# The order of VectorE's work in a time-mix stage, and a rotary cross product as one GpSimd operation

## The chip, the core and the metric

The kernel runs on one core of one Trainium2 chip. Its engines run side by side, each in the order of its own program: PE (matmuls), DVE (VectorE), ACT (ScalarE), POOL (GpSimd) and SP, which here only issues DMAs. They wait for one another through semaphores. The metric is the device time of the launch in microseconds (us), the median of several runs. Times below that look like 1041.29 are us from the start of the profiled span.

## What is computed

One sequence x of 2048 tokens by 128 channels, float32, goes through two parts:

```python
x = layernorm(x + time_mix(x))        # RWKV-6: a recurrence with a decay per channel, 2 heads of 64
x = layernorm(x + layers(x))          # 6 layers of local attention and a gated MLP

# time_mix: y_t = r_t S + (r_t u k_t) v_t ;  S = exp(-exp(w_t)) S + k_t v_t ;  then a norm by head, a gate, @ Wo
# each of the 6 layers, 16 heads of 64, window 32:
q = l2norm(q) * q_scale ; k = l2norm(k) * k_scale
q = q * cos * scale + rotate_half(q) * sin * scale      # k with 1 / scale
x = softmax(8 q k', masked to the window) v @ Wo + x
x = a * gelu(gate) @ W2 + b2 + x
```

rotate_half swaps the two halves of each head's 64 channels and changes the sign of one. The sign lies in the kernel's table of sines, so what is left is a product of each half with a table, written to the other half's place.

## The kernel before

All data stay in SBUF. There are three blocks of code: time_mix (up to about 205 us), layers (up to about 2015 us) and last_norm.

**time_mix** works on 4 groups of 512 tokens (4 chunks of 128). Its loop has 6 steps, and one step treats up to three groups at once: m, whose inputs are mixed and projected; g = m - 1, whose coefficients within a chunk are made level by level; and e = m - 2, whose outputs are made, normed, gated and added. Each engine has this step written out by hand in one order, and that order is what the first part of the change touches on DVE (lines 515 to 624). The operations that matter, in DVE's order before:

- scale_level(g, 0) to (g, 6), L492 to L498: r, k and the decays are scaled for the next level. PE multiplies level by level (L650), so they alternate. Behind level 6 PE transposes k (L794), ACT copies it with the far coefficients (L455 to L457), and PE makes the products that are added to the states (L808).
- stream(0) to (4), L504; cut, L554: the levels' products by masks, 2 x 768 elements.
- y_sum, y_c, y_var, y_eps, y_n, y_w, y_g (L531 to L571): the norm and gate of group e. PE turns y_g (L774), ACT copies it, PE multiplies by Wo (L799).
- res, res_sum, res_c (L576 to L582): the output of e plus x, less its mean. It waits for PE's L799.
- coef (L590): two sums over the levels of cut. PE needs them in the next step (L718).
- gate (L595): from ACT's gate_t (L438). POOL makes gate_w and gate_b from it (L383), and PE may write the bank again.
- res_var, res_eps (L600, L603): from ACT's squares (L461). POOL takes them to the power -0.5 (L377).
- mixed_input(m + 1): xx and x_mixed (L509, L513), the input of the next group. The first matmuls of PE's next step (L687, L689) read it; the first also waits until ACT's rate (L442) has read the bank.
- state (L617), 8 operations: the 4 chunks' states one after the other. They wait for PE's L808. PE's levels 0 and 1 of the next step overwrite the banks that the states read, so they wait for all 8.
- x_tok (L622): the normed output of e. PE turns it (L680) in the next step, after levels 0 and 1.

**layers** works on 96 tiles (6 layers by 16 tiles of 128 tokens), software-pipelined: in step s the projections of tile p = s + 1, the scores of tile a = s and the outputs of tile b = s - 1. The MLP takes two tiles together, so odd and even steps differ, and the unrolled loop holds one of each. For a tile PE projects q and k (L1282, L1297); ACT squares them (L1056); DVE sums (L1153), makes the inverse roots in nine small operations (L88 to L104) and multiplies, unit[0] and unit[1] (L1178). PE's v projection (L1354) overwrites q's bank, so it waits for unit[0]. DVE's root operations come behind heads_out (L1159), which waits for PE's L1316 of tile b. Of the rotation, POOL makes for q: across in two halves (L1000), along (L1034), rotated (L1008); then for k: across, rotated; DVE makes k's along (L1236). POOL goes on with the next table, turns (L1019), and the shifted inputs (L988, L989, L1027, L1028). PE transposes rotated (L1249). One order of POOL for all of it; `cross` and `add_turned` are the two functions that the second part touches.

Of the kernel before, what the change touches and what calls it, by code (L numbers as in the profile page):

```python
# [26 lines left out]
ALU = mybir.AluOpType  # L27
ACT = mybir.ActivationFunctionType
AX = mybir.AxisListType
# [36 lines left out]
def after(engine, semaphore, count):  # L66

    if not isinstance(count, int) or count > 0:
        engine.wait_ge(semaphore, count)
# [124 lines left out]
def time_mix(nc, ctx, given):  # L194
# [20 lines left out]
    with ExitStack() as own:  # L215
# [105 lines left out]
        with nc.Block() as block:  # L321
# [147 lines left out]
            def _(dve):  # L469
# [30 lines left out]
                def step(m, g, e):  # L500
# [71 lines left out]
                    if g is not None:  # L572
                        scale_level(g, 6)
                    if e is not None:
# [10 lines left out]
                    if g is not None:  # L585
                        dve.wait_ge(s_cut, 2 * g + 2)
                        after(dve, s_y, g)
                        for pair in range(2):
                            part = slice(4 * pair, 4 * pair + 4)
                            dve.tensor_reduce(coef[:, part, :], cut[:, part, :, :].rearrange("p a l t -> p a t l"),  # L590
                                              AX.X, ALU.add).then_inc(s_coef, 1)
                    if m is not None:
                        dve.wait_ge(s_gt, m + 1)
                        after(dve, s_gb, m)
                        dve.scalar_tensor_tensor(gate[:, :, :], gate_t[:, :, :], 1.0,  # L595
                                                 slots[:, 1, :].rearrange("p (c d) -> p c d", c=CHUNKS_G),
                                                 ALU.add, ALU.mult).then_inc(s_gate, 1)
                    if e is not None:
                        dve.wait_ge(s_rsq, e + 1)
                        dve.tensor_reduce(res_var[:, :], res_sq[:, :, :], AX.X, ALU.add).then_inc(s_rvar, 1)  # L600
                        dve.wait_ge(s_rvar, e + 1)
                        after(dve, s_pow2, e)
                        dve.tensor_scalar(res_eps[:, :], res_var[:, :], LN_EPS, None, ALU.add).then_inc(s_reps, 1)  # L603
                    if m is not None and m + 1 < GROUPS:
                        mixed_input(m + 1)
                    if g is not None:
# [3 lines left out]
                        for c in range(CHUNKS_G):  # L610
# [3 lines left out]
                            for h in range(R_HEADS):  # L614
# [4 lines left out]
                                                         ALU.mult, ALU.add).then_inc(s_state, 1)  # L619
                    if e is not None:  # L620
# [933 lines left out]
```

## Time and profile before

| | |
|---|---|
| median of 3 runs | 2035.73 us (2034.1 to 2036.3) |
| the profiled execution | 2036.49 us, of it 2034.7 in the span |
| PE | 1804.0 us busy (89%) |
| DVE | 1578.9 us busy (78%) |
| POOL | 1480.6 us busy (73%) |
| ACT | 1163.4 us busy (57%) |
| POOL across (L1000) | 384 operations of 128x512, 524.6 us, mean 1386 ns |
| POOL rotated (L1008) | 192 operations of 128x1024, 495.8 us, mean 2582 ns |
| PE waits for POOL's rotated | 56.1 us, 51 times |
| PE's v projection waits for DVE's unit | 24.2 us, 47 times |

A line of a timeline gives the start, the time taken, the engine, the line of code, the operation and what it writes and reads; "x8" means that eight like it in a row are put together. In square brackets stands how long the engine had been idle before it and what ended that: "[6.08 <-DVE x_mixed L513]" is 6.08 us of idle time that ended when DVE's line 513 was done. "issue" means that the profile shows nothing that it waited for. A share of busy time doesn't say which engine sets the pace where all of them wait for each other in turn; for that one follows who released whom.

### The profile page before, as it was taken

To read this page: it belongs to the slowest core of one execution; us is meant where nothing else is said; L and a number is where in the kernel's file an instruction comes from. 1 tells how busy PE (TensorE), PEld (TensorE's weight loads), DVE (VectorE), ACT (ScalarE), POOL (GpSimd) and SP (SyncE) were. 2 spreads that over 40 slices of the span, in tenths; PEclk is the share of its full clock that TensorE was granted. 3 is DMA by queue.
4 is the path that set the end of the run, shared out by engine and by line. 5 is a ranking of instruction groups with operands and counts; after the bars stand their busy time and mean duration, and the time that the engine had idled before them with its cause. 6 is when DMAs were issued, how large, how long until landed. Compare 5 with 4: busy or idle time off the path is not lost. (4 is left out here: it accounts for less than half of the span.)

```text
span 2034.7 us, 85964 instructions
## 1 busy us (share of the span) xinstructions
PE 1804.0 (89%) x34280; PEld 1309.1 (64%) x34280; DVE 1578.9 (78%) x2776; ACT 1163.4 (57%) x1966; POOL 1480.6 (73%) x1159
## 2 busy tenths in 40 slices
PE   7774689999999999999999999999999999999985
PEld 3443367767666667666666666666766666666664
DVE  3665588888888888888888888888888888888874
ACT  2221356656666666666666666656656666666663
POOL 3221588788887887888877878788788877887871
PEclk8786799999999999999999999999999999999998
DMA  4000122223222223222223222223222232222220
GB/s 148 2 3 1 42 61 61 55 58 93 66 64 56 62 58 83 66 73 59 54 53 93 66 68 53 61 62 91 63 63 62 54 84 68 73 56 52 57 62 22
DMA packets 93581, 123.43 MB, mean 61 GB/s; under 512 B 27760, under 2 KB 41808, under 8 KB 93392
## 3 DMA queue, kind: packets, MB, share of 16 engines
q1 hardware_dynamic: 93232, 122.42, 23.9%
q8 instruction: 46, 0.75, 0.2%
q10 hardware_dynamic: 288, 0.13, 0.0%
q14 instruction: 15, 0.12, 0.0%
HBM read 20.74 MB, written 1.05 MB: 11 GB/s over the span
## 5 line engine op out<-in xcount | busy, mean ns | idle before, releaser
L1000 POOL TENSOR_TENSOR across<-unit,turns 128x512 f32<-128x512 f32 x384 | 524.6, 1386 | 266.1 <-issue 254.5
L1008 POOL TENSOR_TENSOR rotated<-along,across 128x1024 f32<-128x1024 f32 x192 | 495.8, 2582 | 20.4 <-POOL along L1034 9.6
L1153 DVE TENSOR_REDUCE sums<-squares 128x16 f32<-128x1024 f32 x192 | 234.1, 1219 | 157.3 <-ACT squares L1056 151.2
L1249 PE MATMUL turn<-identity,rotated 128*128 128x128 f32 x1536 | 205.0, 277 | 56.1 <-POOL rotated L1008 56.1
L1249 PEld LDWEIGHTS turn<-identity,rotated 128*128 128x128 f32 x1536 | 172.5, 141 | 118.7 <-issue 101.5
L1034 POOL TENSOR_TENSOR along<-unit,turns 128x1024 f32<-128x1024 f32 x96 | 227.3, 2368 | 0.0
L1354 PE MATMUL proj_a<-w_qkv,shift_a 128*128 128x512 f32 x384 | 190.1, 618 | 34.3 <-DVE unit L1178 24.2
L1115 ACT COPY val<-proj_a 128x1024 f32<-128x1024 f32 x96 | 97.2, 1012 | 179.2 <-PE proj_a L1354 179.2
L1091 ACT COPY k_t<-turn 128x512 f32<-128x512 f32 x192 | 103.2, 589 | 155.0 <-PE turn L1249 155.0
L1379 PEld LDWEIGHTS att<-o_t,w_o 128*128 128x128 f32 x1536 | 186.4, 192 | 6.0 <-issue 1.0
L1282 PE MATMUL proj_a<-w_qkv,shift_a 128*128 128x512 f32 x384 | 183.5, 601 | 4.3 <-POOL shift_a L988 3.0
L1379 PE MATMUL att<-o_t,w_o 128*128 128x128 f32 x1536 | 186.9, 275 | 0.0
L1236 DVE TENSOR_TENSOR along<-unit,turns 128x1024 f32<-128x1024 f32 x96 | 182.8, 1904 | 0.0
L1297 PE MATMUL proj_b<-w_qkv,shift_a 128*128 128x512 f32 x384 | 181.1, 594 | 0.0
L1056 ACT ACTIVATE squares<-proj_a 128x1024 f32<-128x1024 f32 x96 | 98.3, 1024 | 114.2 <-PE proj_a L1282 114.2
L1342 PEld LDWEIGHTS turn<-k_t,q_t 64*32 64x32 f32 x12288 | 129.0, 105 | 42.1 <-issue 41.8
L1316 PE MATMUL att<-v_win,p_t 64*32 64x64 f32 x12288 | 154.1, 225 | 0.8 <-ACT p_t L1076 0.8
L1076 ACT COPY p_t<-att 128x512 f32<-128x512 f32 x192 | 103.2, 589 | 89.8 <-PE att L1249 89.8
L1316 PEld LDWEIGHTS att<-v_win,p_t 64*32 64x32 f32 x12288 | 135.9, 105 | 19.6 <-issue 17.1
L1159 DVE TENSOR_TENSOR heads_out<-att,inv_mass 128x512 f32<-128x512 f32 x192 | 123.6, 686 | 29.7 <-PE att L1316 29.7
L1342 PE MATMUL turn<-k_t,q_t 64*32 64x64 f32 x12288 | 145.1, 227 | 0.1
L1170 DVE TENSOR_TENSOR logits<-turn,row_max 128x512 f32<-128x512 f32 x192 | 132.7, 691 | 6.6
(203 smaller groups left out, 3448.9 us busy)
## 6 DMA issues: line engine op xcount, KB each, us to landing
v_win<-val SPq DMA_DIRECT2D x1536, 64.0 KB, 2.0
w_qkv<-wqkv_dram SPq DMA_DIRECT2D x18, 512.0 KB, 4.0
w_o<-wo_dram SPq DMA_DIRECT2D x6, 512.0 KB, 5.2
where<-positions_dram SPq DMA_DIRECT2D x1, 2048.0 KB, 10.2
w_ffn<-ffn_dram SPq DMA_DIRECT2D x12, 170.5 KB, 2.3
w_ffn<-ffn_dram SPq DMA_DIRECT2D x6, 192.0 KB, 2.3
x_tok<-x_dram SPq DMA_DIRECT2D x4, 256.0 KB, 4.2
out_dram<-final SPq DMA_DIRECT2D x4, 256.0 KB, 2.4
```

Of the source, the lines that this page charges most:

```text
L1000: pool.tensor_tensor(a[:, :, 1 - half, :], u[:, :, half, :], table, ALU.mult)\
L1008: pool.tensor_tensor(rotated[j][:, :, :], along[j][:, :, :], across[j][:, :, :], ALU.add).then_inc(rotated_in[j], 1)
L1034: pool.tensor_tensor(along[0][:, :, :], unit[0][:, :, :], turns[mine][:, 0, :].unsqueeze(1).broadcast_to([128, HEADS, HEAD]), ALU.mult).th ...
L1153: dve.tensor_reduce(sums[:, j, :], squares[j][:, :, :], AX.X, ALU.add).then_inc(summed[j], 1)
L1236: dve.tensor_tensor(along[1][:, :, :], unit[1][:, :, :], turns[mine][:, 2, :].unsqueeze(1).broadcast_to([128, HEADS, HEAD]), ALU.mult).the ...
L1249: mm = pe.transpose(bank[:, TILE * (i % 4):TILE * (i % 4) + TILE], buffer[:, TILE * i:TILE * i + TILE], identity[:, :])
L1282: mm = pe.matmul(bank_a[:, half, :], shift_a[mine][:, :], w_qkv[:, 512 * half:512 * half + 512], start=True, stop=True)
L1297: mm = pe.matmul(bank_b[:, half, :], shift_a[mine][:, :], w_qkv[:, base:base + 512], start=True, stop=True)
L1316: mm = pe.matmul(bank_s[WINDOW * w:WINDOW * w + WINDOW, par, HEAD * a_:HEAD * a_ + HEAD], p_t[rows, a_, WINDOW * w:WINDOW * w + WINDOW], v ...
L1342: mm = pe.matmul(bank_t[WINDOW * w:WINDOW * w + WINDOW, par, HEAD * a_:HEAD * a_ + HEAD], q_t[rows, a_, WINDOW * w:WINDOW * w + WINDOW], k ...
L1354: pe.matmul(bank_a[:, par, :].rearrange("p (a e) -> p a e", a=PAIRS), shift_a[mine][:, :], values[:, par, :, :], start=True, stop=True).th ...
L1379: mm = pe.matmul(bank_s[:, 0, 0:TILE], w_o[:, a_, :], o_t[:, a_, :], start=(a_ == 0), stop=(a_ == PAIRS - 1))
```

## The change

Two parts. In time_mix's step DVE makes coef ahead of scale_level(g, 6) and, behind that level, mixed_input(m + 1) and gate; then res, res_sum and res_c; then the states; and res_var and res_eps come behind the states, directly ahead of x_tok. In layers' rotation the two halves of across become one operation on 1024 elements, whose output is written with the two halves in reverse order; its semaphore rises by 1 for a tile instead of 2, and the waits on it are changed to match.

```diff
--- before.py
+++ after.py
@@ -570,7 +570,22 @@
                         after(dve, s_yturn, e)
                         dve.tensor_tensor(y_g[:, :, :], y_w[:, :, :], gate_b[e % 2][:, :, :], ALU.add).then_inc(s_yg, 1)
                     if g is not None:
+                        dve.wait_ge(s_cut, 2 * g + 2)
+                        after(dve, s_y, g)
+                        for pair in range(2):
+                            part = slice(4 * pair, 4 * pair + 4)
+                            dve.tensor_reduce(coef[:, part, :], cut[:, part, :, :].rearrange("p a l t -> p a t l"),
+                                              AX.X, ALU.add).then_inc(s_coef, 1)
+                    if g is not None:
                         scale_level(g, 6)
+                    if m is not None and m + 1 < GROUPS:
+                        mixed_input(m + 1)
+                    if m is not None:
+                        dve.wait_ge(s_gt, m + 1)
+                        after(dve, s_gb, m)
+                        dve.scalar_tensor_tensor(gate[:, :, :], gate_t[:, :, :], 1.0,
+                                                 slots[:, 1, :].rearrange("p (c d) -> p c d", c=CHUNKS_G),
+                                                 ALU.add, ALU.mult).then_inc(s_gate, 1)
                     if e is not None:
                         dve.wait_ge(s_out, e + 1)
                         dve.tensor_tensor(res[:, :, :], turn[:, 1, :].rearrange("p (c d) -> p c d", c=CHUNKS_G),
@@ -582,27 +597,6 @@
                         dve.scalar_tensor_tensor(res_c[:, :, :],
                                                  res_sum[:, :].unsqueeze(2).broadcast_to([128, CHUNKS_G, DIM]),
                                                  -1.0 / DIM, res[:, :, :], ALU.mult, ALU.add).then_inc(s_rc, 1)
-                    if g is not None:
-                        dve.wait_ge(s_cut, 2 * g + 2)
-                        after(dve, s_y, g)
-                        for pair in range(2):
-                            part = slice(4 * pair, 4 * pair + 4)
-                            dve.tensor_reduce(coef[:, part, :], cut[:, part, :, :].rearrange("p a l t -> p a t l"),
-                                              AX.X, ALU.add).then_inc(s_coef, 1)
-                    if m is not None:
-                        dve.wait_ge(s_gt, m + 1)
-                        after(dve, s_gb, m)
-                        dve.scalar_tensor_tensor(gate[:, :, :], gate_t[:, :, :], 1.0,
-                                                 slots[:, 1, :].rearrange("p (c d) -> p c d", c=CHUNKS_G),
-                                                 ALU.add, ALU.mult).then_inc(s_gate, 1)
-                    if e is not None:
-                        dve.wait_ge(s_rsq, e + 1)
-                        dve.tensor_reduce(res_var[:, :], res_sq[:, :, :], AX.X, ALU.add).then_inc(s_rvar, 1)
-                        dve.wait_ge(s_rvar, e + 1)
-                        after(dve, s_pow2, e)
-                        dve.tensor_scalar(res_eps[:, :], res_var[:, :], LN_EPS, None, ALU.add).then_inc(s_reps, 1)
-                    if m is not None and m + 1 < GROUPS:
-                        mixed_input(m + 1)
                     if g is not None:
                         dve.wait_ge(s_add, g + 1)
                         dve.wait_ge(s_scaled, 3 * LEVELS * (g + 1))
@@ -617,6 +611,12 @@
                                 dve.scalar_tensor_tensor(new[part, part], old[part, part], decay[LEVELS - 1][part, c:c + 1],
                                                          chunk_bank(c)[part, at:at + R_HEAD],
                                                          ALU.mult, ALU.add).then_inc(s_state, 1)
+                    if e is not None:
+                        dve.wait_ge(s_rsq, e + 1)
+                        dve.tensor_reduce(res_var[:, :], res_sq[:, :, :], AX.X, ALU.add).then_inc(s_rvar, 1)
+                        dve.wait_ge(s_rvar, e + 1)
+                        after(dve, s_pow2, e)
+                        dve.tensor_scalar(res_eps[:, :], res_var[:, :], LN_EPS, None, ALU.add).then_inc(s_reps, 1)
                     if e is not None:
                         dve.wait_ge(s_pow2, e + 1)
                         dve.tensor_tensor(x_tok[:, CHUNKS_G * e:CHUNKS_G * e + CHUNKS_G, :], res_c[:, :, :],
@@ -994,16 +994,14 @@
                     pool.wait_ge(united[j], p + 1)
                     after(pool, rotated_in[j], p)
                     u, a = halves(unit[j]), halves(across[j])
-                    for half in range(2):
-                        table = turns[odd][:, 2 * j + 1, 32 * half:32 * half + 32].unsqueeze(1).broadcast_to(
-                            [128, HEADS, 32])
-                        pool.tensor_tensor(a[:, :, 1 - half, :], u[:, :, half, :], table, ALU.mult)\
-                            .then_inc(acrossed[j], 1)
+                    table = turns[odd][:, 2 * j + 1, :].rearrange("p (two e) -> p two e", two=2).unsqueeze(1)\
+                        .broadcast_to([128, HEADS, 2, HEAD // 2])
+                    pool.tensor_tensor(a[:, :, ::-1, :], u, table, ALU.mult).then_inc(acrossed[j], 1)
 
                 def add_turned(j, p):
 
                     pool.wait_ge(alonged[j], p + 1)
-                    pool.wait_ge(acrossed[j], 2 * p + 2)
+                    pool.wait_ge(acrossed[j], p + 1)
                     after(pool, (q_turned, k_turned)[j], 2 * p)
                     pool.tensor_tensor(rotated[j][:, :, :], along[j][:, :, :], across[j][:, :, :],
                                        ALU.add).then_inc(rotated_in[j], 1)
@@ -1014,7 +1012,7 @@
                     p, mine = s + 1, 1 - odd
                     if live["p"]:
                         after(pool, alonged[1], p - 1)
-                        after(pool, acrossed[1], 2 * (p - 1))
+                        after(pool, acrossed[1], p - 1)
                         after(pool, alonged[0], p - 1)
                         pool.tensor_tensor(turns[mine][:, :, :], where[:, tile_of(p), :, :], scales[:, layer_of(p), :, :],
                                            ALU.mult).then_inc(table_made, 1)
@@ -1174,7 +1172,7 @@
                     def unite(j):
                         dve.wait_ge(rooted, ROOT_OPS * p + ROOT_OPS)
                         after(dve, alonged[j], p)
-                        after(dve, acrossed[j], 2 * p)
+                        after(dve, acrossed[j], p)
                         dve.tensor_tensor(unit[j][:, :, :], by_head((bank_a, bank_b)[j]),
                                           inv_norm[:, j, :].unsqueeze(2).broadcast_to([128, HEADS, HEAD]),
                                           ALU.mult).then_inc(united[j], 1)
```

## Rows read from the trace of the kernel before

**Rows 1.** Windows view, layers: stretch, length, busy us of each engine (instructions).

```profile
300.00:1980.00 1680.00, 1567.22 (x30254) 1155.06 (x30252) 1378.26 (x2372) 1060.06 (x1778) 1360.26 (x1049) 1.00 0.26 65
```

**Rows 2.** Timeline, PE, layers: start us, us, engine, line, operation, out<-in, count [idle before].

```profile
1027.30 1.96 PE L1354 MATMUL proj_a<-w_qkv,shift_a 128*128 128x512 f32 x4 [0.61 <-DVE unit L1178]
1041.29 1.09 PE L1249 MATMUL turn<-identity,rotated 128*128 128x128 f32 x8 [0.99 <-POOL rotated L1008]
1043.83 1.49 PE L1342 MATMUL turn<-k_t,q_t 64*32 64x64 f32 x128
1045.40 1.53 PE L1354 MATMUL proj_a<-w_qkv,shift_a 128*128 128x512 f32 x3
```

**Rows 3.** Timeline, DVE, layers: the first tiles and two steady tiles.

```profile
231.11 2.29 DVE L88 SCALAR_TENSOR_TENSOR sums_min<-sums 128x32 f32<-128x32 f32 x1
...
1007.22 1.22 DVE L1178 TENSOR_TENSOR unit<-proj_a,inv_norm 128x1024 f32<-128x1024 f32 x1
...
1040.51 1.29 DVE L1159 TENSOR_TENSOR heads_out<-att,inv_mass 128x512 f32<-128x512 f32 x2 [0.30 <-PE att L1316]
1042.16 0.32 DVE L92 TENSOR_TENSOR root_work<-inv_norm 128x32 f32<-128x32 f32 x1
1043.08 0.19 DVE L98 SCALAR_TENSOR_TENSOR inv_norm<-root_work,inv_norm 128x32 f32<-128x32 f32 x1
1044.08 1.23 DVE L1178 TENSOR_TENSOR unit<-proj_a,inv_norm 128x1024 f32<-128x1024 f32 x1
```

**Rows 4.** Timeline, POOL, layers, the same steady tiles.

```profile
1042.15 0.28 POOL L988 COPY shift_a<-xa 64x128 f32 x1 [0.30 <-POOL turns L1019]
1045.44 2.49 POOL L1000 TENSOR_TENSOR across<-unit,turns 128x512 f32<-128x512 f32 x2 [2.66 <-issue]
1047.89 2.37 POOL L1034 TENSOR_TENSOR along<-unit,turns 128x1024 f32<-128x1024 f32 x1
```

**Rows 5.** View of one line (L383): line, engine, operation, count: ns min/median/max, starts; form.

```profile
L383 POOL TENSOR_TENSOR gate_w<-gate,half_rows x4: 1261/1453/1657, 26.9 to 144.7; 128x512 f32<-128x512 f32 x4
```

**Rows 6.** Timeline, PE, first stage: operations behind the long idle stretches.

```profile
29.11 1.22 PE L687 MATMUL att<-x_mixed,w 128*128 128x512 f32 x1 [2.63 <-DVE x_mixed L513]
...
103.83 1.22 PE L687 MATMUL att<-x_mixed,w 128*128 128x512 f32 x1 [6.08 <-DVE x_mixed L513]
...
146.29 0.34 PE L650 MATMUL proj_a<-rf_bonus,kf 64*32 64x32 f32 x14 [6.04 <-DVE state L617]
...
147.81 0.48 PE L680 MATMUL turn<-identity,x_tok 128*128 128x128 f32 x1
...
169.04 0.48 PE L794 MATMUL proj_a<-identity,kf 128*128 128x128 f32 x1 [0.99 <-DVE decay L498]
...
180.84 0.48 PE L680 MATMUL turn<-identity,x_tok 128*128 128x128 f32 x1 [7.48 <-DVE x_tok L622]
```

**Rows 7.** Timeline, DVE, first stage, the step m=2, g=1, e=0 and the next step's start.

```profile
86.42 0.69 DVE L571 TENSOR_TENSOR y_g<-y_w,gate_b 128x512 f32<-128x512 f32 x1
89.44 0.42 DVE L492 TENSOR_TENSOR rf<-rf,decay 128x256 f32<-128x256 f32 x1 [2.32 <-PE proj_b L781]
...
98.18 2.81 DVE L590 TENSOR_REDUCE coef<-cut 128x128 f32<-128x768 f32 x2
104.94 1.22 DVE L617 SCALAR_TENSOR_TENSOR state<-state,decay,proj_b 64x64 f32<-64x64 f32 x4
106.19 0.69 DVE L622 TENSOR_TENSOR x_tok<-res_c,rstd 128x512 f32<-128x512 f32 x1
108.90 0.43 DVE L492 TENSOR_TENSOR rf<-rf,decay_one 128x256 f32<-128x256 f32 x1 [2.02 <-PE proj_b L650]
```

**Rows 8.** Timeline, ACT, first stage: rate in step m=0, the copies of far in step m=1.

```profile
26.52 0.69 ACT L442 ACTIVATE rate<-att,vec 128x512 f32<-128x512 f32 x1 [0.46 <-PE att L790]
...
55.28 0.52 ACT L455 COPY far<-proj_a 32x128 f32<-32x128 f32 x2
```

**Rows 9.** Timeline, POOL, first stage: the power behind the variance of res, step m=3.

```profile
143.73 1.02 POOL L377 TENSOR_TENSOR rstd<-res_eps,minus_half 128x4 f32<-128x4 f32 x1 [17.26 <-DVE res_eps L603]
```

## The prediction

> **What bounds the kernel now.** I read three views. First the busy times by stretch: in the layers PE is busy 93% of the time, at a granted clock of 1.00 [rows 1]. Its gaps are small, so the question is which of them set the pace. That is read from the engines' timelines over two tiles, one after the other; the pattern repeats every 36.86 us, which is two tiles: DVE's first unit operation starts at 1007.22 and again at 1044.08, with the one of the other tile between them [rows 3].
>
> Follow the loop that closes. PE projects v at 1045.40, 0.09 after DVE's first unit operation ends (1044.08 + 1.23 = 1045.31) [rows 2, 3]. From there PE runs almost without a gap to the products of probabilities and values. In the tile before, their end is what releases DVE's division (heads_out) at 1040.51, after 0.30 of idle; then come nine small root operations and unit at 1044.08 [rows 3], and PE's next v projection waits for that. In the other tile the same wait is seen as 0.61 of idle PE behind unit [rows 2]. So the pace is PE -> heads_out -> root -> unit -> PE, and **POOL is not in this loop**.
>
> POOL seems to be in it: PE waits 0.99 for the rotated keys at 1041.29 [rows 2]. But what follows that wait, the score products, ends at 1043.83 + 1.49 = 1045.32, and the v projection behind it waits for unit until 1045.31 anyway. The two chains meet within 0.1 us. If POOL is earlier, PE idles the same time a little further on; if POOL is later by more than 0.1, it sets the pace.
>
> The first stage, which lasts to about 205 us, is another matter: each engine waits for the others in turn. PE stands idle for 2.63, 6.08, 6.04 and 7.48 us in front of operations that wait for x_mixed, x_mixed, the states and x_tok [rows 6]. All four are DVE's, and DVE makes all four behind work that nobody waits for yet. That is what the first part of the change moves.
>
> **Part 1, DVE's order in the first stage.** A step treats three groups of 512 tokens at once: m (inputs), g (levels), e (outputs). The same instructions are issued as before; only their order changes, with the waits that they have. No DMA, PE, ACT or POOL instruction moves. Step by step (m = 0, 1, 2, 3, none, none):
>
> Step m=0. x_mixed of group 1 was made behind gate and released PE at 29.11 [rows 6]. It now comes ahead of gate, in an idle stretch of DVE, and is ready before gate was. PE's first product must still wait until rate has left its bank: ACT's rate runs from 26.52 to 27.21 [rows 8]. So PE starts at about 27.3 instead of 29.1: **-1.8**. The bounds are 1.5 and the whole idle, 2.6.
>
> Step m=1. Here the coefficient sums (2.81 for the two [rows 7]) come ahead of level 6, whose keys PE transposes for ACT to copy. But ACT starts these copies at 55.28 with no idle before them, right behind its other work [rows 8], so most of the delay is covered. I take **+0.2** for what sticks out; if no cover held it would be up to 2. x_mixed of group 2 is early here too, but PE had no gap at that place.
>
> Step m=2. DVE ends y_g at 86.42 + 0.69 = 87.11 and level 6 started at 89.44, after PE had released it [rows 7]. The sums fill this hole: 87.1 + 2.8 = 89.95, level 6 is 0.5 late, and its transposes come later than that anyway, since two PE products lie ahead of them. Then x_mixed of group 3 is ready at about 92.2, gate at 92.9, and res to res_c stay where they are, since they wait for PE; they end where the sums began, at 98.2 [rows 7]. Now the states follow at once: PE had their products done at 103.83 - 6.08 = 97.75 [rows 6]. They take 2 x 1.25 [rows 7]: 98.25 to 100.75. Then the variance of res (0.7 + 0.2), POOL's power (1.0 [rows 9]) and x_tok (0.69 [rows 7]): 103.45. DVE's level 0 of the next step started at 108.90 [rows 7] and now starts at 103.45. PE, which no longer waits at 97.75, has its two input products and levels 0 and 1 done at 102 to 103, and then waits for x_tok to turn it. That turn stood at about 108.8 and is at 103.5: **-5.3**. Thus the 6.08 of idle is not all won: what is late next is x_tok, whose power on POOL used to hide beside the states and now is bare. Bounds 4.3 and 6.1.
>
> Step m=3. There is no further input. PE had the states' products done at 146.29 - 6.04 = 140.25 [rows 6]. States 140.3 to 142.8, variance to 143.7, power to 144.7, x_tok to 145.45. PE turned x_tok at 147.81 [rows 6], now at 145.5: **-2.3**. The levels alone could start 3.5 earlier; again x_tok is last. Bounds 1.5 and 3.5.
>
> Step g=3. PE waits here for level 6 already (0.99 of idle at 169.04 [rows 6]), so the sums ahead of it cost their 0.5 in full, in the output products and in res. What DVE then leaves out between res_c and x_tok is the 2.8 of sums; but the power, 1.0, comes bare: 2.8 - 1.1 - 0.5 = 1.2, and rounding the semaphores down, **-1.1** on the turn that stood at 180.84 [rows 6]. Bounds 0.5 and 1.7. The last step has nothing that moved.
>
> Sum of part 1: -1.8 + 0.2 - 5.3 - 2.3 - 1.1 = **-10.3**. PE's clock goes up and down in this stage; I count nothing for that, and 2 either way in the range.
>
> **Part 2, the cross product as one operation.** It takes out one of two POOL operations, twice in each of 96 tiles, and one semaphore increment. A pair spans 2.49, and the along operation next to it, with as many elements as both halves (1024) and a broadcast table too, takes 2.37 [rows 4]. So a merged operation should save 0.12. No row shows its exact form, with three free dimensions and one of them backwards. The nearest: a half (16 runs of 32) takes half of 2.49 plus the overlap, some 1.26, and gate_w, of as many elements in 4 runs of 128, takes 1.261 at its quickest [rows 5]. So the number of runs costs nothing, and I take 2.37. The bounds are 2.3 and, if something in the form costs, 2.37 x 1.5 = 3.5.
>
> Twice 0.12 puts POOL's second rotated 0.25 earlier, and by the loop above that is worth nothing: PE waits 0.74 instead of 0.99 for the keys, and longer for unit. Two small things are left. POOL's copy of shift_a (0.28) lies over the root operations, and DVE's root operation at 1042.16 takes 0.32 beside it, where one behind it takes 0.19 [rows 3, 4]; two root operations a tile are hit so, 0.13 each, and these are on the loop. Moved up by 0.25, the copies still lie over root operations. What each hit costs depends on which starts first, so a part of the 0.26 may go in one of the two tiles: 0 to 0.2 for each pair of tiles, times 44 pairs (48 less the filling): 0 to -9, and I take **-2**. And while the layers fill, in the first tiles, DVE's root operation waits out POOL's rotated operation (2.29 instead of 0.19 at 231.11 [rows 3]), so POOL is on the path there: two times 0.12 in a tile or two, **-0.5**.
>
> A longer operation also holds DVE off for longer. The Trainium skill (SBUF — State Buffer, section "Who interferes with whom") says that POOL and a DVE operation with two SBUF inputs exclude each other for a whole instruction. By that rule a DVE operation issued under the merged product can wait 2.37 where it waited 1.26. The wait at 231.11 agrees with it. In the steady tiles no such DVE operation is issued while a cross product runs, so by the rule nothing would be added there.
>
> **Sum.** The profiled execution took 2036.49 (span 2034.7), the median is 2035.73. 2036.49 - 10.3 - 2 - 0.5 = 2023.7; from the median the same 12.8 gives **2022.9**.
>
> **The rivals.**
> *The stage gives back.* Group 0 to 3 are chained by many waits, and I followed only those that I saw end last. If in two of the steps another wait ends next, 4 or so is left of 10.3: 2035.7 - 5 = 2031. For it: x_tok turns up as next in three steps already. Against: the idle stretches are long and the moved operations have their inputs.
> *POOL's wait is the pace.* If PE's 0.99 at 1041.29 was the true limit, each pair of tiles gains 0.25: 44 x 0.25 = 11, and the time is 2012. Against it stands the meeting of the two chains at 1045.3.
> *The copies leave the root operations.* 0.2 for each pair: 9 instead of 2, the time is 2016.
> *The merged product is slower than the pair* (the other side). For y more than 2.49 each, two lie in a row in POOL's chain, which has 0.1 of slack in every second tile. The cost is 44 x (2y - 0.1); it eats the 10.8 of the rest from y = 0.17 on, a merged operation of 2.66. At 3.5, y = 1.0, it is +84: 2109; at y = 0.3 it is +22: 2047. For it: the form is unseen. Against: runs cost nothing in the rows. The Trainium skill (GPSIMD Engine Reference, section 7) has a rule of +50% for reads whose step is over 8 bytes; by its words it doesn't bite, since the innermost step stays 4 bytes and the backward step is in the output, and no run so far shows more.
> *The merge saves nothing* (2.49 as before): the fill and the copies stay, and the time is 2025, inside my forecast.
>
> **How the numbers follow.** Forecast, with the last of these: 0.60. Gain in the steady tiles by POOL's pace or by the copies: 0.08 and 0.10. Stage gives back: 0.14, of which half lies within 0.2%. Slower product: 0.08. A difference of 0.2% (4 us) is about what a measurement of this kernel can tell from none. Faster by more than that: 0.60 + 0.18 + 0.07 = 0.85, less 0.01 for a slightly slow product: 0.84; same 0.08; slower 0.08. The range leaves out the slower product and the far ends: 2012 to 2031.
>
> **What would show it.** On PE's timeline the idle at 103.83 and 29.11 must be gone, and before the turns of x_tok a few tenths to one us must stand instead of 6 and 7. POOL's across must be 192 operations of 2.37. PE's wait for rotated must shrink by some 10 us in total and its wait for unit grow by about as much, with a period of 36.86 less at most 0.2. A period that falls by 0.25 with PE's wait for unit unchanged proves me wrong on the loop; one that grows says that the product is slow.

## The result: a gain of twice the size

The changed kernel takes 2010.68 us (median of 4 runs, 2006.95 to 2013.87), the kernel before 2034.91 beside it. The ratio is 0.988, with a 95% interval from 0.9863 to 0.9897: faster by 24.2 us. 2022.9 was predicted, with a range down to 2012.

Where the time went is read from three marks: when DVE's first and last unit operations start, and when the span ends. The view of the tile unit gives the first two: line, operation, count: ns min/median/max, first and last start; form. First the kernel before, then the changed one.

```profile
L1178 DVE TENSOR_TENSOR unit<-proj_a,inv_norm x96: 1223/1225/1226, 218.8 to 1965.7; 128x1024 f32<-128x1024 f32 x96
```

```profile
L1176 DVE TENSOR_TENSOR unit<-proj_a,inv_norm x96: 1224/1224/1226, 208.6 to 1938.7; 128x1024 f32<-128x1024 f32 x96
```

The first stage gave 10.2 (218.8 to 208.6). The 96 tiles of the layers went from 1746.9 to 1730.1: 16.8. What follows the last unit went from 69.0 (2034.7 - 1965.7) to 72.0 (2010.7 - 1938.7): 3.0 were lost there. The sum, 24.0, is the difference of the two spans. The forecast for the stage was 10.3, the one for the layers 2.5 and the one for the end 0. **The miss lies in the layers.** The start of the first unit is not a sharp measure of the first stage: it is 217.4 to 219.9 in the four kernels with the old stage (mean 219.0) and 207.4 to 212.8 in the seven executions with the new one (mean 209.7), which makes 9.3 of the 10.2.

The page of the changed kernel, its lines on what the change touched:

```profile
span 2010.7 us, 85596 instructions
PE 1805.9 (90%) x34280; PEld 1311.9 (65%) x34280; DVE 1557.0 (77%) x2776; ACT 1164.3 (58%) x1966; POOL 1455.2 (72%) x967
L999 POOL TENSOR_TENSOR across<-unit,turns 128x1024 f32<-128x1024 f32 x192 | 497.4, 2591 | 279.7 <-issue 268.4
L1247 PE MATMUL turn<-identity,rotated 128*128 128x128 f32 x1536 | 205.2, 277 | 36.4 <-POOL rotated L1006 36.4
L1352 PE MATMUL proj_a<-w_qkv,shift_a 128*128 128x512 f32 x384 | 189.9, 617 | 36.4 <-DVE unit L1176 30.1
```

across is 192 operations of 497.4 us instead of 384 of 524.6. The view of the tile across gives the spread, ns min/median/max:

```profile
L999 POOL TENSOR_TENSOR across<-unit,turns x192: 2342/2356/3349, 210.0 to 1948.0; 128x1024 f32<-128x1024 f32 x192
```

The median is 2.36, as for the plain along operation (2.37 [rows 4]), so the form with three free dimensions and one backwards costs nothing here. The mean of 2591 ns comes from k's product in every second tile, which takes 3.34 there; the half in its place took 2.25 instead of 1.26 before as well. PE's wait for rotated fell from 56.1 to 36.4, and its wait for unit rose from 24.2 to 30.1.

**The first stage.** On PE's timeline of the changed kernel stand the operations of [rows 6]:

```profile
27.39 1.10 PE L687 MATMUL att<-x_mixed,w 128*128 128x512 f32 x2 [0.87 <-ACT rate L442]
...
55.94 1.92 PE L687 MATMUL att<-x_mixed,w 128*128 128x512 f32 x2
...
91.67 1.02 PE L687 MATMUL att<-x_mixed,w 128*128 128x512 f32 x2
...
98.21 1.11 PE L680 MATMUL turn<-identity,x_tok 128*128 128x128 f32 x4 [2.41 <-DVE x_tok L622]
...
139.56 1.12 PE L680 MATMUL turn<-identity,x_tok 128*128 128x128 f32 x4 [2.17 <-DVE x_tok L622]
...
171.18 1.11 PE L680 MATMUL turn<-identity,x_tok 128*128 128x128 f32 x4 [5.62 <-DVE x_tok L622]
```

The first product waits for rate at 27.39, as forecast at 27.3. The 6.08 of idle in front of x_mixed at 103.83 is gone. What is late next is x_tok, as forecast, but by 2.41 and not by some tenths. DVE and POOL at that place:

```profile
94.38 0.69 DVE L616 TENSOR_REDUCE res_var<-res_sq 128x4 f32<-128x512 f32 x1
95.10 0.17 DVE L619 TENSOR_SCALAR res_eps<-res_var 128x4 f32<-128x4 f32 x1
96.41 1.75 DVE L622 TENSOR_TENSOR x_tok<-res_c,rstd 128x512 f32<-128x512 f32 x1 [1.14 <-POOL rstd L377]
98.08 1.49 DVE L492 TENSOR_TENSOR rf<-rf,decay_one 128x256 f32<-128x256 f32 x1
```

```profile
95.35 1.02 POOL L377 TENSOR_TENSOR rstd<-res_eps,minus_half 128x4 f32<-128x4 f32 x1 [17.31 <-DVE res_eps L619]
96.35 1.26 POOL L383 TENSOR_TENSOR gate_w<-gate,half_rows 128x512 f32<-128x512 f32 x1
97.56 1.72 POOL L383 TENSOR_TENSOR gate_b<-gate,half_rows 128x512 f32<-128x512 f32 x1
```

The power is bare for 1.14. Then x_tok takes 1.75 instead of 0.69, and the next scaling 1.49 instead of 0.42 or 0.43. POOL had sat idle for 17 us, and its program puts the two gate operations behind the power, so they start exactly when DVE wants x_tok. Run 9 tests whether they are what holds DVE up.

### The profile page after: what moved, and what is told of

Read it like the earlier page. It is cut to its first block and busy times, and to the rows that moved or that the text cites. A ratio compares the mean times of both kernels' runs of the same rounds, so it can differ in the third digit from the quotient of the medians.

```text
span 2010.7 us, 85596 instructions
## 1 busy us (share of the span) xinstructions
PE 1805.9 (90%) x34280; PEld 1311.9 (65%) x34280; DVE 1557.0 (77%) x2776; ACT 1164.3 (58%) x1966; POOL 1455.2 (72%) x967
## 3 DMA queue, kind: packets, MB, share of 16 engines
q1 hardware_dynamic: 93232, 122.42, 24.2%
## 5 line engine op out<-in xcount | busy, mean ns | idle before, releaser
L999 POOL TENSOR_TENSOR across<-unit,turns 128x1024 f32<-128x1024 f32 x192 | 497.4, 2591 | 279.7 <-issue 268.4
L1247 PE MATMUL turn<-identity,rotated 128*128 128x128 f32 x1536 | 205.2, 277 | 36.4 <-POOL rotated L1006 36.4
L1352 PE MATMUL proj_a<-w_qkv,shift_a 128*128 128x512 f32 x384 | 189.9, 617 | 36.4 <-DVE unit L1176 30.1
L1234 DVE TENSOR_TENSOR along<-unit,turns 128x1024 f32<-128x1024 f32 x96 | 166.4, 1733 | 0.0
L1054 ACT ACTIVATE squares<-proj_a 128x1024 f32<-128x1024 f32 x96 | 98.3, 1024 | 114.2 <-PE proj_a L1280 114.2
```

Of the source, the lines that this page charges most:

```text
L999: pool.tensor_tensor(a[:, :, ::-1, :], u, table, ALU.mult).then_inc(acrossed[j], 1)
L1234: dve.tensor_tensor(along[1][:, :, :], unit[1][:, :, :], turns[mine][:, 2, :].unsqueeze(1).broadcast_to([128, HEADS, HEAD]), ALU.mult).the ...
L1247: mm = pe.transpose(bank[:, TILE * (i % 4):TILE * (i % 4) + TILE], buffer[:, TILE * i:TILE * i + TILE], identity[:, :])
L1352: pe.matmul(bank_a[:, par, :].rearrange("p (a e) -> p a e", a=PAIRS), shift_a[mine][:, :], values[:, par, :, :], start=True, stop=True).th ...
```

## The experiments

Ten runs. All times are medians beside runs of the kernel before, which had 2035.17, 2034.47 and 2036.01 in the three groups. "Period" is the time of two tiles, from the starts of unit in tile 10 and in tile 90, divided by 40; it is 36.86 before and 36.48 in the changed kernel.

**1. Only DVE's order.** The kernel before with the change's time_mix; the rotation as before.

> Only DVE's new order in the first stage; the cross product stays in two halves. If the first stage's gain is that of the prediction, DVE's first unit operation in the layers starts 10.2 us earlier (218.85 before, 208.61 after), the period of two tiles stays 36.86 us, and the time is about 2034.9 - 10 = 2025. Rival: the earlier start moves the layers into another rhythm, and the period falls by itself; then the time is below 2015 and the period near 36.5.

Measured: 2026.29, ratio 0.9959 (0.9945 to 0.9973). First unit at 210.7 (208.6 was expected), last at 1957.8, period 36.87. So an earlier start does not change the layers' rhythm, and this part alone gives 9 in the median. The marks are those of the profiled execution, which was the longest of the five (2031.77).

**2. Only the merged cross product.** The kernel before with the change's layers.

> Only the merged cross product, with DVE's order of before. If the two parts add up, the first unit stays at 218.8, the period is 36.48 instead of 36.86, and with 44 pairs of tiles the time is 2034.9 - 17 = 2018. Rival (the prediction's): the merge is worth 0 to 0.2 a pair, the time is above 2025.

Measured: 2018.19, ratio 0.9916 (0.9898 to 0.9934), period 36.48. The parts add up to within 2 us: 8.9 and 17.0 alone, 24.2 together. The prediction's 0 to 0.2 for each pair of tiles is refuted; it is 0.38.

**3. Two halves, counted once.** What else has the merge changed? A tile's cross product raised its semaphore twice, so others waited for 2p; now it is p. This run has the halves of before and the count of after:

```diff
-                        pool.tensor_tensor(a[:, :, 1 - half, :], u[:, :, half, :], table, ALU.mult)\
-                            .then_inc(acrossed[j], 1)
+                        product = pool.tensor_tensor(a[:, :, 1 - half, :], u[:, :, half, :], table, ALU.mult)
+                    product.then_inc(acrossed[j], 1)
...
-                        after(dve, acrossed[j], 2 * p)
+                        after(dve, acrossed[j], p)
```

> The kernel before, with one edit: the cross product stays in two halves, but only the second half raises the semaphore, so that the waits on it are for p and not for 2p. Theory of the count: to wait for 2p an engine must work out 2p in a register, and this register operation lies between the end of DVE's last root operation and unit (0.13 us between them before, 0.03 after), and between POOL's along and rotated (0.22 before, 0.08 after). Then here too the gap before unit is 0.03, 0.1 in each of 96 tiles, and POOL is 0.1 to 0.2 earlier; the period falls from 36.86 to 36.6 or less, and the time to 2034.9 - 9 = 2026 or less. Rival, the operation's length alone: nothing changes, 36.86 and 2035.

Measured: 2022.10, ratio 0.9933 (0.9917 to 0.995), period 36.55. **With not one POOL operation shortened, 0.31 of the 0.38 is there.** DVE's timeline shows the gap in front of unit, first in the kernel before (1043.76 + 0.19 = 1043.95, then 0.13 until the 1044.08 of [rows 3]), then in this run (1021.52 + 0.19 = 1021.71, then 0.04):

```profile
1043.76 0.19 DVE L104 SCALAR_TENSOR_TENSOR inv_norm<-root_work,inv_norm 128x32 f32<-128x32 f32 x1
```

```profile
1021.52 0.19 DVE L104 SCALAR_TENSOR_TENSOR inv_norm<-root_work,inv_norm 128x32 f32<-128x32 f32 x1
1021.75 1.22 DVE L1178 TENSOR_TENSOR unit<-proj_a,inv_norm 128x1024 f32<-128x1024 f32 x1
```

What went is a register operation: a small instruction in the engine's queue that works out a number, here the count to wait for. Line 69 is the helper `after`; its register operations on DVE's and POOL's queues, before and then in this run:

```profile
L69 POOLq ALU_OP  x176: 32/35/45, 356.4 to 1955.0; - x176
L69 DVEq ALU_OP  x132: 45/45/50, 362.7 to 1965.6; - x132
```

```profile
L69 POOLq ALU_OP  x132: 32/35/39, 360.8 to 1943.3; - x132
L69 DVEq ALU_OP  x44: 45/45/50, 375.3 to 1947.2; - x44
```

88 fewer on DVE: one for each tile of the rolled loop. In the eight tiles that are written out ahead of the loop p is a plain number and there is nothing to work out. They are a control within the trace of the kernel before: in all eight the gap is 0.03, and in the 88 of the loop 0.13. The fourth tile, before:

```profile
272.63 0.19 DVE L104 SCALAR_TENSOR_TENSOR inv_norm<-root_work,inv_norm 128x32 f32<-128x32 f32 x1
272.86 1.22 DVE L1178 TENSOR_TENSOR unit<-proj_a,inv_norm 128x1024 f32<-128x1024 f32 x1
```

The operation itself takes 45 ns, but it starts only behind the last root operation, and unit behind it. Line 69 on DVE's queue within the gap, before (1043.95 to 1044.08):

```profile
L69 DVEq ALU_OP  x1: 45/45/45, 1044.0 to 1044.0; - x1
```

The gap is shorter by 0.094 in each tile (0.128 before, 0.034 here), which is 0.19 of the 0.31. The other 0.12 are root operations that POOL's copies now lengthen less (3.78 us a pair instead of 3.90; means of tiles 10 to 89), since POOL too has lost a register operation.

**4. Merged, counted twice.** The opposite half of the change: one operation that raises the semaphore by 2, and waits for 2p.

```diff
+                    pool.tensor_tensor(a[:, :, ::-1, :], u, table, ALU.mult).then_inc(acrossed[j], 2)
```

> The merged cross product with DVE's order of before, but the one operation raises the semaphore by 2 and all waits are for 2p as before. Theory of the count: the gap before unit stays 0.13; POOL's second rotated ends 0.25 earlier, and what is left of the gain is that of the copies beside the root operations, 0 to 0.2 a pair: a period of 36.66 to 36.86, and 2026 to 2035. Rival, the operation's length alone: the period is 36.48 and the time 2018, as with the merged product that counts by one.

Measured: 2025.44, ratio 0.9953 (0.9934 to 0.9971), period 36.64, both just beyond the better end of what was expected.

```profile
1020.58 0.19 DVE L92 TENSOR_TENSOR root_work<-inv_norm 128x32 f32<-128x32 f32 x1
1020.80 0.29 DVE L94 TENSOR_TENSOR root_work<-root_work,sums_min 128x32 f32<-128x32 f32 x1
...
1022.02 0.19 DVE L104 SCALAR_TENSOR_TENSOR inv_norm<-root_work,inv_norm 128x32 f32<-128x32 f32 x1
1022.34 1.23 DVE L1176 TENSOR_TENSOR unit<-proj_a,inv_norm 128x1024 f32<-128x1024 f32 x1
```

The gap is 0.13 as before (1022.21 to 1022.34). One root operation of the tile is lengthened by 0.1 where there were two by 0.13. All root operations of a pair take 0.22 less than before, which is the whole fall of the period. So POOL's being earlier is worth 0.22 a pair by the copies alone, a little over the upper end of the prediction's 0 to 0.2, and its shorter product in itself nothing. The runs 3 and 4 give 0.31 and 0.22 of 0.38: they don't add up, since both move POOL's copies and a root operation can be freed of a copy only once.

**5. The same count put on another semaphore.** The changed kernel, in which along counts by two: both of its increments are 2, and the other waits on it are doubled like the one shown.

```diff
-                        after(dve, alonged[j], p)
+                        after(dve, alonged[j], 2 * p)
```

> The changed kernel, with the same double count put onto the other semaphore: along raises its semaphore by 2, and the waits on it are for 2p. Theory of the count: the gap between DVE's last root operation and unit goes from 0.03 back to 0.13 in each tile, 0.2 a pair, and POOL's rotated starts some 0.1 later behind along; the period is 36.6 to 36.8 and the time 6 to 15 us above the changed kernel's, 2017 to 2026. Rival, the gain came from the length alone: 36.48 and 2011.

Measured: 2025.01, ratio 0.9944 (0.9928 to 0.9961), period 36.83; the changed kernel in the same group 2010.81. 14 lost by a factor of two in a wait.

```profile
1018.52 0.19 DVE L104 SCALAR_TENSOR_TENSOR inv_norm<-root_work,inv_norm 128x32 f32<-128x32 f32 x1
1018.91 1.22 DVE L1176 TENSOR_TENSOR unit<-proj_a,inv_norm 128x1024 f32<-128x1024 f32 x1 [0.20 <-DVE inv_norm L104]
```

The direction is that of the theory, the size isn't: the gap is 0.20 and not 0.13, and the period is 36.83, just above the 36.6 to 36.8 expected. POOL's rotated did not come later behind along. DVE's queue shows two instructions of line 69 in the gap (1018.72 to 1018.90), where there was one in the kernel before:

```profile
L69 DVEq ALU_OP  x1: 45/45/45, 1018.8 to 1018.8; - x1
L69 DVEq EVENT_SEMAPHORE  x1: 21/21/21, 1018.8 to 1018.8; - x1
```

So what a worked-out count costs depends on where it falls among the other waits: in the kernel before, the wait for the other semaphore, along's, lay ahead of the register operation; here the one for across lies behind it. Over a gap of 0.034, one instruction in it cost 0.09 a tile (0.128) and two cost 0.16 (0.197).

**6. POOL's copies away from the root operations.** The changed kernel; ACT makes the two shift_a copies, ahead of its squares.

```diff
-                    pool.tensor_copy(shift_a[odd][0:64, :], xa[0:64, columns(m)]).then_inc(shifted, 1)
-                    pool.tensor_copy(shift_a[odd][64:128, :], xa[64:128, columns_before(m)]).then_inc(shifted, 1)
+                    act.copy(shift_a[odd][0:64, :], xa[0:64, columns(m)]).then_inc(shifted, 1)
+                    act.copy(shift_a[odd][64:128, :], xa[64:128, columns_before(m)]).then_inc(shifted, 1)
```

> The changed kernel, with the two shift_a copies of each tile made by ACT, in its idle place ahead of the squares, instead of by POOL beside DVE's root operations. In the changed kernel three root operations of each two tiles are lengthened, by 0.09, 0.05 and 0.13 (0.28, 0.24 and 0.32 us instead of 0.19). Theory that POOL's copies hold them up: all are 0.19 now, and the period falls by 0.27, from 36.48 to 36.21; with 46 pairs the time is 12 us less than the changed kernel's, about 1998. Rival: the lengthening has another cause, or PE's chain through the rotated keys, which then ends only 0.05 before unit does, sets the pace; the period stays within 0.1 of 36.48.

Measured: 1994.29, ratio 0.9794 (0.9777 to 0.981), period 36.21, against 2010.81 for the changed kernel in the same group. In the changed kernel DVE's and POOL's timelines show a root operation stretched by a copy:

```profile
1043.45 0.32 DVE L92 TENSOR_TENSOR root_work<-inv_norm 128x32 f32<-128x32 f32 x1
```

```profile
1043.43 0.29 POOL L989 COPY shift_a<-xa 64x128 f32 x1
```

and with the copies on ACT the same operation on DVE, and the copies on ACT's:

```profile
1035.88 0.19 DVE L92 TENSOR_TENSOR root_work<-inv_norm 128x32 f32<-128x32 f32 x1
```

```profile
1028.80 0.30 ACT L1039 COPY shift_a<-xa 64x128 f32 x1
1029.12 0.29 ACT L1040 COPY shift_a<-xa 64x128 f32 x1
```

The stretched operation ends 0.05 after the copy (1043.77 after 1043.72). The period met the expected 36.21; the time fell by 16.5 where 12 was expected. By the marks of the two profiled executions 13.2 of it lie in the layers; the rest lies ahead of them and behind them, where the code is the same (first unit at 207.4, and 68.7 behind the last one). **This version beats both kernels.**

**7. The same with the cross product in halves again.** What is POOL's length itself worth?

```diff
-                    pool.tensor_tensor(a[:, :, ::-1, :], u, table, ALU.mult).then_inc(acrossed[j], 1)
...
+                        product = pool.tensor_tensor(a[:, :, 1 - half, :], u[:, :, half, :], table, ALU.mult)
+                    product.then_inc(acrossed[j], 1)
```

> As the version with the copies on ACT, but the cross product in two halves again, that raise the semaphore once. This asks what POOL's length itself is worth when no copy can meet the root operations. The prediction's loop says that POOL's chain had 0.1 of slack in every second tile, and the version with ACT's copies leaves 0.05. POOL's second rotated ends 0.25 later here, so the period is 0.2 longer than that version's, about 36.4, and the time about 2006. Rival: the chain has more slack than that, and the two are equal.

Measured: 2009.95 (2006 was expected), ratio 0.9872 (0.9855 to 0.9888), period 36.44, first unit at 210.1, 70.8 behind the last one. PE's timeline, and DVE's unit at that place:

```profile
1024.39 1.09 PE L1247 MATMUL turn<-identity,rotated 128*128 128x128 f32 x8 [0.95 <-POOL rotated L1000]
1026.93 1.48 PE L1340 MATMUL turn<-k_t,q_t 64*32 64x64 f32 x128
1028.42 1.96 PE L1352 MATMUL proj_a<-w_qkv,shift_a 128*128 128x512 f32 x4
```

```profile
1026.87 1.22 DVE L1176 TENSOR_TENSOR unit<-proj_a,inv_norm 128x1024 f32<-128x1024 f32 x1
```

unit ends at 1028.09, but PE's score products end at 1028.41, and the v projection starts behind them without a wait. Here, and in none of the other runs, POOL's rotated sets the pace in every second tile. That POOL's chain has hardly any slack is confirmed, though with the copies away it was less than the 0.05 expected: 0.25 more in this chain cost 0.23 a pair. A merged product is worth nothing by its length in the kernel before (run 4), and 10.8 us of the layers once DVE's loop is shortened (1727.8 against 1717.0 from the first unit to the last). The other 4.9 of the 15.7 between the two times lie outside the layers, where the two kernels have the same code.

**8. The changed kernel again.**

> The changed kernel again, as the measure for the three others on the same chip: 2011 within 4, a period of 36.48, every theory alike.

Measured: 2010.81 (2004.31 to 2013.41), period 36.49, first unit at 209.4.

**9. POOL's gate operations ahead of the power.** On the version of experiment 6, to test what held x_tok up.

```diff
-                    if e is not None:
-                        pool.wait_ge(s_reps, e + 1)
-                        after(pool, s_one, e)
-                        pool.tensor_tensor(rstd2[:, :], res_eps[:, :], minus_half[:, 0:CHUNKS_G], ALU.pow)\
-                            .then_inc(s_pow2, 1)
                     if m is not None:
                         pool.wait_ge(s_gate, m + 1)
...
+                    if e is not None:
+                        pool.wait_ge(s_reps, e + 1)
+                        after(pool, s_one, e)
+                        pool.tensor_tensor(rstd2[:, :], res_eps[:, :], minus_half[:, 0:CHUNKS_G], ALU.pow)\
+                            .then_inc(s_pow2, 1)
```

> The version with the copies on ACT, and one edit in the first stage: POOL makes gate_w and gate_b ahead of the power for x_tok instead of behind it. In the changed kernel x_tok takes 1.75 us and the next level's first scaling 1.49, where they take 0.69 and 0.42 alone: POOL's two gate operations run just then. Theory that they hold DVE up: both are back at 0.69 and 0.42 in the steps m=2 and m=3, 2.1 us each, of which 1.1 is in front of PE's turn of x_tok; the first unit operation starts 2 to 4 us earlier than in the version without the edit, and the time is 2 to 4 less. Rival: what PE's clock does with the saved idle time outweighs it, and the difference is within 1.

> The version with the copies on ACT again, as the measure for the one with the gates first: 1994 within 3, the first unit operation at about 207.5.

Measured: 1994.43 (ratio 0.98, 0.9787 to 0.9814) with the edit, 1997.80 (0.9809, 0.9794 to 0.9825) without; the latter is the kernel of run 6, which had 1994.29 there, and was expected at 1994 within 3. DVE's timeline with the edit:

```profile
95.78 0.69 DVE L622 TENSOR_TENSOR x_tok<-res_c,rstd 128x512 f32<-128x512 f32 x1 [1.14 <-POOL rstd L384]
96.39 0.42 DVE L492 TENSOR_TENSOR rf<-rf,decay_one 128x256 f32<-128x256 f32 x1
```

x_tok and the scaling are back at 0.69 and 0.42: POOL's two gate operations are what lengthened them. The first unit starts at 204.1 instead of 209.0. How much of these 4.9 is the edit's can't be told: the start of the first unit differs by over 5 us between kernels with an identical first stage (207.4 to 212.8 with the changed one). The medians differ by 3.4, inside the expected 2 to 4, but their intervals overlap, so a gain of the whole kernel is not shown.

## Why the prediction was wrong, step by step

**The loop: right.** The prediction said that PE -> heads_out -> root -> unit -> PE sets the pace and POOL doesn't. Follow DVE around it. From the start of unit to the first root operation of the next tile, in which PE's part of the loop and heads_out lie, it takes as long in the changed kernel as before. The first two lines are of the kernel before (15.75), the others of the changed one (15.73):

```profile
1025.97 1.23 DVE L1178 TENSOR_TENSOR unit<-proj_a,inv_norm 128x1024 f32<-128x1024 f32 x1
1041.72 0.18 DVE L88 SCALAR_TENSOR_TENSOR sums_min<-sums 128x32 f32<-128x32 f32 x1
...
1008.67 1.23 DVE L1176 TENSOR_TENSOR unit<-proj_a,inv_norm 128x1024 f32<-128x1024 f32 x1
1024.40 0.18 DVE L88 SCALAR_TENSOR_TENSOR sums_min<-sums 128x32 f32<-128x32 f32 x1
```

In the mean over the tiles 10 to 89 this stretch is 15.72 in one tile and 16.43 in the other, and within 0.02 of that in the changed kernel and in the runs 1 to 6 and 8. Only in run 7 is it longer, 16.68 in every second tile. So the fall of the period is all in the root operations and in the gap behind them, which are DVE's part of the loop.

The signs that the prediction wrote down did worse. It wanted a period shorter by at most 0.2, and PE's waits to move by some 10 us each; the period fell by 0.38, the wait for rotated by 19.7, and the wait for unit grew by 5.9. What was to refute the loop, a period shorter by 0.25 with the wait for unit unchanged, didn't come in that form either: the period fell by more, and the wait grew. It was a bad test, since it took for granted that the change leaves DVE's part of the loop alone. In the changed kernel the loop is still in place:

```profile
1023.57 1.09 PE L1247 MATMUL turn<-identity,rotated 128*128 128x128 f32 x8 [0.59 <-POOL rotated L1006]
...
1026.11 1.48 PE L1340 MATMUL turn<-k_t,q_t 64*32 64x64 f32 x128
1027.84 1.96 PE L1352 MATMUL proj_a<-w_qkv,shift_a 128*128 128x512 f32 x4 [0.25 <-DVE unit L1176]
```

PE's 0.99 in front of rotated is 0.59, and 0.25 in front of unit is new where there was none [rows 2]: most of what POOL gave moved to the next wait, as forecast.

**The wait for unit: the step that failed.** "It takes out one of two POOL operations ... and one semaphore increment." The increment was costed at nothing, as a thing of POOL's. But the diff also has `after(dve, acrossed[j], 2 * p)` becoming `p`, on DVE, in front of unit, in the very loop that I had found. I didn't cost the waits at all. The gap of 0.13 between the last root operation and unit could be read from the trace of before, beside gaps of 0.03 between the root operations; I took the nine operations and unit as one piece and never asked what the gap was. It was 0.09 in each of 88 tiles: some 8 us, put at nothing.

**The copies beside the root operations: right in kind, too small in size.** The term was 0 to 0.2 a pair, 0.04 taken. Two things moved POOL: the shorter products (0.25), and the register operation between along and rotated, which was on POOL's queue as well, 0.14 more (the gap there was 0.22 and is 0.08). Together POOL's copies came 0.4 earlier in one of the two tiles. There the root operations took 0.17 less in all, in the other one 0.03 less: 0.20 a pair, some 9 us, at the upper end that I had written and over four times what I took. A value near the lower end had no reason for it: nothing on record said which of two operations starts first.

**Sum for the layers:** 0.19 for the gaps and 0.20 for the root operations a pair, 44 pairs: 17. Measured 16.8. The measured time lies 1.3 us below the range; without the 3.0 lost at the end it would have been 4.3.

**The first stage: the sum right, its terms not.** -10.3 was forecast and 10.2 measured; by where the marks stand, the gain had grown to 1.7 at the first product, to 2.7 at the second (58.67 before, to 55.94), to 10.6 at the first turn of x_tok, fell back to 8.2 at the second, and was 9.7 at the third. So step m=1 gave 1.0 where 0.2 was to be lost, and m=2 gave 7.9 where 5.3 was forecast. Over these steps PE's granted clock was higher (0.92 in the mean over 8 to 98 us, 0.83 before), and its long idle stretches were gone; how much of the difference that explains isn't shown. In m=3 2.4 were lost where 2.3 were to be won. In this step x_tok's wait for POOL's gates shows again, and PE's granted clock was 0.82 from 98 to 132, where it had been 0.95 from 108 to 140. This loss is one execution's reading: from the first turn of x_tok to the second it takes 39.0 to 42.2 in the four kernels with the old stage and 39.1 to 44.1 in the seven executions with the new one. The prediction has gate ready at 92.9 and doesn't follow POOL from there. It passed over POOL's own order, in which the power stands in front of the gate operations: a step that is moved on one engine moves with it what is queued behind it on another. That the total came out within 0.1 is luck twice over: the terms were wrong both ways, and the end of the same stage lies over 5 us apart from one run to another.

**The end.** 3.0 were lost after the last unit. The code there is the same. Over this stretch PE's granted clock was 0.86 in the kernel before and 0.80 in the changed one:

```profile
1966.00:2034.00 68.00, 41.92 (x668) 0.86 0.13 32
```

```profile
1939.00:2010.00 71.00, 46.34 (x651) 0.80 0.12 31
```

Of the other executions with the new first stage, those of the runs 1, 5, 7 and 8 and the edited one of run 9 lost 1.5 to 3.2 there too (70.5 to 72.2, at a granted clock of 0.79 to 0.84), and the two of run 6's kernel lost nothing (68.7, at 0.86). So the loss goes with the clock; the new first stage alone doesn't bring it. Why the clock is lower there in some of them isn't settled.

**The rivals.** "The merged product is slower" is refuted by its 2.36. "The copies leave the root operations" (2016, 0.10) was the mechanism for half of the layers' gain. "POOL's wait is the pace" (2012) has the nearest number and the wrong reason: by run 4 the shorter product alone is worth only what the copies give, and the stretch through PE kept its length. "The stage gives back" isn't what the sum shows: 10.2 were left and not 4 or so. The price of a wait's count was in no rival.

## What to carry to other kernels

When a loop of waits sets the pace, take the gaps between its operations as seriously as the operations, and cost the waits in a diff like instructions: here a count that must be worked out from a loop variable (2p instead of p) cost 0.09 to 0.16 us each time at the place where the last wait ends. Let a semaphore count once for each iteration. And when one operation is moved earlier, follow the program of every engine that waits for it: what is queued behind that wait comes at a new time, and may meet the next step at its worst moment.

## What the runs showed of the hardware that I had not expected

- A register operation of 45 ns that stands between the last root operation and unit costs 0.09 us (2p on one semaphore: a gap of 0.128 against 0.034, the kernel before and run 3), or 0.16 with a wait of 21 ns behind it (2p on another: 0.197, run 5), and leaves no trace in an engine's busy time.
- A POOL product written with three free dimensions, the middle one backwards, takes 2.36 for 1024 elements, as the plain one does (2.37).
- A DVE operation of 0.19 with two inputs in SBUF, started 0.02 after a POOL copy of 0.29, takes 0.32: it ends 0.05 after the copy. Two such copies a tile on POOL cost 0.27 a pair of tiles, 12 us of this kernel, by that alone; on ACT they don't lengthen the loop (run 6).
